# Slot steps of a fused transformer kernel: the feed-forward's norm on VectorE, the bias product behind the up product, activation tables loaded ahead

## The chip, the cores and the metric

The kernel is one program on one core of one Trainium2 chip. The metric is the device time of a run in microseconds (us), from first to last instruction with the launch around it. Before the change three runs gave 2456.42, 2447.18 and 2455.42 us; their median is 2455.42 us.

## The reference, cut to what matters

The whole reference is slot attention over a context, a routed mixture of experts, six transformer layers and a quantised feed-forward. Only the first part is touched. There 4 batches of 512 tokens of width 128 (the "slots") pass three times through this body:

```python
q = _ln(slots, lnq_g, lnq_b) @ wq + bq
logits = jnp.einsum('bnd,bkd->bnk', k, q) / scale
attn = jax.nn.softmax(logits, axis=-1) + EPS_ATTN
attn = attn / jnp.sum(attn, axis=1, keepdims=True)
upd = jnp.einsum('bnk,bnd->bkd', attn, v)
slots = upd @ wu + bu + prev
h = _ln(slots, lnm_g, lnm_b) @ w1 + b1
slots = jax.nn.gelu(h, approximate=False) @ w2 + b2 + slots
slots = _ln(slots + x_cls[:, None, :], lnp_g, lnp_b)
```

All of it is float32. The products with `wu` and the additions of `bu`, `b2` and `x_cls` are folded into prepared values (`slot_v`, `cond_rows`).

## The kernel before

`slot_steps` is unrolled: three steps (`s`), four batches (`b`), four tiles of 128 tokens per batch (`TB`). Each engine has its own in-order program, and semaphores that count up by one per batch tie them together: a wait holds everything behind it on that engine. The order within an engine is written out by hand as small software pipelines, `for k in range(B + 1 or B + 2)`, in which stage one works on batch `k`, stage two on `k - 1`, stage three on `k - 2`.

A step has two halves. In the **query half** TensorE turns the normalised state (`turn`, L311), multiplies with `wq` (L316) and with the keys (L320); ScalarE applies gain and offset (`gain`, L366), the query bias (L371) and the exponential (L375); VectorE takes the maximum and divides; TensorE makes the update (L327).

In the **feed-forward half**, which the change touches:

- VectorE's `add_update(s, b)` divides and adds the update (L488, L493) and takes the moments of the new state (L455 and L458) for all four batches in a row.
- GpSimd's `root_and_shift` makes from the moments of a batch the factor `rstd` (L410 and L413, a power of -0.5) and `shift` = -mean x rstd (L422, L425).
- ScalarE's `normal` (L381) makes `hat` = state x rstd + shift, four instructions per batch; then `gain` (L366) and `gelu` (L387). `normal` of batch `k`, `gain` of `k - 1` and `gelu` of `k - 2` follow each other.
- TensorE runs `turn` of batch `k` (L311), `up` of `k - 1` (L333) and `down` of `k - 2`. `down` waits for the gelu, then issues a product with one row of contraction that writes the bias (`ones32` with `cond_rows`, L337) into PSUM bank `2b`, and on top of it four products (L340). A float32 product is two matmul instructions in the trace.
- VectorE's `add_output` (L500) adds the result to the state and takes moments; GpSimd's `root` and VectorE's `normal` (L124) make the last norm one batch behind, and GpSimd's `last_gain` (L430, L431) applies its gain and offset. In steps 0 and 1 the moments, roots and norms of the next query (`query_moments`, `root`, `normal`) are woven in.

ScalarE holds one set of function tables at a time. The exponential and the gelu are in different sets, and the compiler puts an ACT_TABLE_LOAD in front of the first activation that needs another set; Identity needs none.

Of the kernel before, what the change touches and what calls it, by code (L numbers as in the profile page):

```python
# [14 lines left out]
ALU = mybir.AluOpType  # L15
# [275 lines left out]
def slot_steps(nc, a, m, sem):  # L291
# [13 lines left out]
    with nc.Block() as block:  # L305
        @block.tensor
        def _(pe):
            def turn(s, b, hat, turned):
                pe.wait_ge(hat, count(s, b))
                for t in range(TB):  # L310
                    last = nc.tensor.transpose(m.ps[:, 2 * b, t * P:(t + 1) * P], m.hat[:, b * TB + t, :], m.ident[:])  # L311
                last.then_inc(turned, 1)

            def queries(s, b):
                pe.wait_ge(in_q, count(s, b))
                nc.tensor.matmul(m.ps[:, 2 * b + 1, :], m.mats0[:, 2, :], m.xnT[:, b, :], start=True, stop=True).then_inc(q_ps, 1)  # L316

            def similarities(s, b):
                pe.wait_ge(q_sb, count(s, b))
                nc.tensor.matmul(m.ps[0:N_CTX, 2 * b, :], m.slot_k[:, b * N_CTX:(b + 1) * N_CTX], m.qT[:, b, :],  # L320
                                 start=True, stop=True).then_inc(logits, 1)

            def update(s, b):
                pe.wait_ge(attn, count(s, b))
                for t in range(TB):
                    bank, at = 2 * b + 1 - t // 2, t % 2 * 2 * P
                    last = nc.tensor.matmul(m.ps[:, bank, at:at + D + 1], m.attn[0:N_CTX, b, t * P:(t + 1) * P],  # L327
                                            m.slot_v[0:N_CTX, b, :], start=True, stop=True)
                last.then_inc(upd, 1)

            def up(s, b):
                pe.wait_ge(in_m, count(s, b))
                nc.tensor.matmul(m.ps[:, 2 * b + 1, :], m.mats0[:, 4, :], m.xnT[:, b, :], start=True, stop=True).then_inc(h_ps, 1)  # L333

            def down(s, b):
                pe.wait_ge(h_sb, count(s, b))
                nc.tensor.matmul(m.ps[:, 2 * b, :], m.ones32[0:1, :], m.cond_rows[0:1, b:b + 1, :].to_broadcast([1, TB, D]),  # L337
                                 start=True, stop=False)
                for t in range(TB):
                    last = nc.tensor.matmul(m.ps[:, 2 * b, t * P:(t + 1) * P], m.qT[:, b, t * P:(t + 1) * P], m.mats0[:, 5, :],  # L340
                                            start=False, stop=(t == TB - 1))
                last.then_inc(out_ps, 1)

            for s in range(SLOT_STEPS):
                for k in range(B + 2):
                    if k < B:
                        turn(s, k, hat_q, turned_q)
                    if 1 <= k <= B:
                        queries(s, k - 1)
                    if k >= 2:  # L350
                        similarities(s, k - 2)
                for b in range(B):
                    update(s, b)
                for k in range(B + 2):
                    if k < B:
                        turn(s, k, hat_m, turned_m)
                    if 1 <= k <= B:
                        up(s, k - 1)
                    if k >= 2:
                        down(s, k - 2)  # L360

        @block.scalar
        def _(act):
            def gain(s, b, turned, column, ready):
                act.wait_ge(turned, count(s, b))
                nc.scalar.activation(m.xnT[:, b, :], m.ps[:, 2 * b, :], ACT.Identity, bias=m.cols0[:, column + 1:column + 2],  # L366
                                     scale=m.cols0[:, column:column + 1]).then_inc(ready, 1)

            def query_bias(s, b):
                act.wait_ge(q_ps, count(s, b))  # L370
                nc.scalar.activation(m.qT[:, b, :], m.ps[:, 2 * b + 1, :], ACT.Identity, bias=m.cols0[:, 8:9]).then_inc(q_sb, 1)  # L371

            def exponentials(s, b):
                act.wait_ge(mx, count(s, b))
                nc.scalar.activation(m.attn[0:N_CTX, b, :], m.ps[0:N_CTX, 2 * b, :], ACT.Exp, bias=m.negmx[0:N_CTX, b:b + 1],  # L375
                                     scale=scale, accum_out=m.psum_rows[0:N_CTX, b:b + 1]).then_inc(probs, 1)

            def normal(s, b):
                act.wait_ge(root_m, count(s, b))
                for t in range(b * TB, (b + 1) * TB):  # L380
                    last = nc.scalar.activation(m.hat[:, t, :], m.state[:, t, :], ACT.Identity, bias=m.shift[:, t:t + 1],  # L381
                                                scale=m.st.rstd[:, t:t + 1])
                last.then_inc(hat_m, 1)

            def gelu(s, b):
                act.wait_ge(h_ps, count(s, b))
                nc.scalar.activation(m.qT[:, b, :], m.ps[:, 2 * b + 1, :], ACT.Gelu, bias=m.cols0[:, 9:10]).then_inc(h_sb, 1)  # L387

            for s in range(SLOT_STEPS):
                for k in range(B + 2):  # L390
                    if k < B:
                        gain(s, k, turned_q, 2, in_q)
                    if 1 <= k <= B:
                        query_bias(s, k - 1)
                    if k >= 2:
                        exponentials(s, k - 2)
                for k in range(B + 2):
                    if k < B:
                        normal(s, k)
                    if 1 <= k <= B:  # L400
                        gain(s, k - 1, turned_m, 4, in_m)
                    if k >= 2:
                        gelu(s, k - 2)

        @block.gpsimd
        def _(pool):
            chain = Chain(pool, pch)

            def add_epsilon(b):
                return nc.gpsimd.tensor_scalar(tiles(m.st.var, b), tiles(m.st.mv, b)[:, :, 1], LN_EPS, None, ALU.add)  # L410

            def power(b):
                return nc.gpsimd.tensor_tensor(tiles(m.st.rstd, b), tiles(m.st.var, b), m.minus_half[:], ALU.pow)  # L413

            def root(s, b, moments, ready):
                pool.wait_ge(moments, count(s, b))
                chain.link(add_epsilon(b))
                power(b).then_inc(ready, 1)

            def root_and_shift(s, b):  # L420
                pool.wait_ge(moments_m, count(s, b))
                nc.gpsimd.tensor_scalar(tiles(m.shift, b), tiles(m.st.mv, b)[:, :, 0], -1.0, None, ALU.mult)  # L422
                chain.link(add_epsilon(b))
                chain.link(power(b))
                nc.gpsimd.tensor_tensor(tiles(m.shift, b), tiles(m.shift, b), tiles(m.st.rstd, b), ALU.mult).then_inc(root_m, 1)  # L425

            def last_gain(s, b):
                pool.wait_ge(hat_p, count(s, b))
                hat = tiles(m.hat, b)
                chain.link(nc.gpsimd.tensor_tensor(hat, hat, m.rows0[:, 2:3, :].to_broadcast([P, TB, D]), ALU.mult))  # L430
                nc.gpsimd.tensor_tensor(tiles(m.state, b), hat, m.rows0[:, 3:4, :].to_broadcast([P, TB, D]), ALU.add).then_inc(gained, 1)  # L431

            for b in range(B):
                root(0, b, moments_q, root_q)
            for s in range(SLOT_STEPS):
                again = s + 1 < SLOT_STEPS
                for b in range(B):
                    root_and_shift(s, b)
                for k in range(B + 2):
                    if k < B:  # L440
                        root(s, k, moments_p, root_p)
                    if again and 2 <= k - 1:
                        root(s + 1, k - 3, moments_q, root_q)
                    if 1 <= k <= B:
                        last_gain(s, k - 1)
                if again:
                    root(s + 1, B - 1, moments_q, root_q)

        @block.vector
        def _(dve):  # L450
# [58 lines left out]
            for s in range(SLOT_STEPS):  # L509
                again = s + 1 < SLOT_STEPS  # L510
                for k in range(B + 1):
                    if k < B:
                        maximum(s, k)
                    if k >= 1:
                        divide(s, k - 1)
                for b in range(B):
                    add_update(s, b)
                for k in range(B + 1):
                    if k < B:
                        add_output(s, k)  # L520
# [1480 lines left out]
def build(nc, a):  # L2001
    with ExitStack() as ctx:
# [46 lines left out]
        m.invsum = {kind: sb(f"invsum_{kind}", [P, TB * 4, 2]) for kind in ("self", "cross")}  # L2049
        m.prefer = sb("prefer", [P, EXPERTS])  # L2050
        m.minus_half = sb("minus_half", [P, TB])
        m.slot_k = early(2400, NC_ALL)
        m.slot_vT = early(2750, NC_ALL)
        m.slot_v = early(3100, B, D + 1)
# [161 lines left out]
```

## Time and profile before

| | |
|---|---|
| median of 3 runs | 2455.42 us (2447.18 to 2456.42) |
| profiled execution | 2452.29 us, its span 2450.6 us |
| mean granted TensorE clock | 0.916 of full |
| busy over the span | PE 83%, PEld 37%, DVE 69%, ACT 63%, POOL 35% |
| DMA | 144.40 MB, mean 59 GB/s |
| ACT_TABLE_LOAD in the slot steps | 5: three before a gelu (L387), two before an exponential (L375) |

The span is that of the one core from its first to its last instruction; the profiled execution lasted 1.7 us more than its span. PE is TensorE's matmuls, PEld its weight loads, DVE VectorE, ACT ScalarE, POOL GpSimd. In a row of the timeline the first number is the start in us from the span's start, the second how long the merged instructions took together, xN their count, and the bracket says how long the engine had been idle before and what ended that.

### The profile page before, as it was taken

How to read it: one execution, taken by the hardware profiler on the slowest of the kernel's cores; microseconds unless marked ns; L12 is line 12 of the kernel's file. 1: busy time of each engine (PE TensorE's matmuls, PEld its weight loads, DVE VectorE, ACT ScalarE, POOL GpSimd, SP SyncE). 2: the span in 40 equal slices, each digit the busy share in tenths (PEclk: the TensorE clock that was granted, in tenths of full speed). 3: DMA queues.
4: the chain of work that ended last, by engine and by line, in shares of the span. 5: the costliest groups of instructions: out<-in, count | busy, mean ns of one | idle time of the engine just before them, and what ended most of it. 6: DMA issues, size and time to landing. Idle time of an engine off the chain costs nothing.

```text
span 2450.6 us, 38334 instructions
## 1 busy us (share of the span) xinstructions
PE 2035.4 (83%) x14066; PEld 899.4 (37%) x14066; DVE 1687.8 (69%) x3124; ACT 1539.8 (63%) x1939; POOL 857.1 (35%) x1354
## 2 busy tenths in 40 slices
PE   2654799926789999999999999999999999987652
PEld 1332576711223333333343333333333333332321
DVE  6776211136778888888878887888878887885455
ACT  1432233303567888788777888788778877867442
POOL 4443000012324444443444445434444445422321
PEclk9776899966999999999999999999999999988765
DMA  1000001032133334333333334333243334311100
GB/s 48 1 0 1 35 1 34 0 77 56 49 67 68 79 89 96 80 74 80 77 82 75 79 89 88 81 81 72 71 83 86 80 89 77 93 36 36 32 5 9
DMA packets 148642, 144.40 MB, mean 59 GB/s; under 512 B 30887, under 2 KB 136163, under 8 KB 148451
## 3 DMA queue, kind: packets, MB, share of 16 engines
q1 hardware_dynamic: 148463, 142.05, 25.9%
q8 instruction: 108, 1.77, 0.3%
q14 instruction: 71, 0.58, 0.1%
HBM read 79.01 MB, written 60.51 MB: 57 GB/s over the span
## 4 chain that ended last, share of the span: by engine, by line
PE 55%; DVE 14%; ACT 5%; issue 3%; POOL 1%; DMA 1%; SPq 0%; POOLq 0%; DVEq 0%; ACTq 0%
PE ps L1263 14%; PE ps L1227 6%; DVE smax L1761 6%; PE ps L1216 6%; PE ps L1341 5%; PE ps L1373 4%; PE ps L1382 4%; PE ps L1275 4%; ACT big L1496 2%; PE ps L1316 2%; DVE rot L1777 2%; PE ps L1300 2%; PE ps L1238 1%; PE ps L1250 1%; PE ps L1333 1%
## 5 line engine op out<-in xcount | busy, mean ns | idle before, releaser
L1496 ACT ACTIVATE big<-ps 128x1024 f32<-128x1024 f32 x960 | 955.4, 1026 | 275.2 <-PE ps L1227 253.5
L1761 DVE TENSOR_REDUCE smax<-ps 128x2 f32<-128x1024 f32 x768 | 921.6, 1221 | 264.2 <-PE ps L1216 258.4
L1263 PE MATMUL ps<-big,vaug 128*32 128x512 f32 x3072 | 414.3, 618 | 3.1 <-ACT big L1496 3.1
L1216 PE MATMUL ps<-k,q 49*128 49x512 bf16 x1536 | 294.3, 391 | 66.3 <-DVE smax L1761 35.4
L1227 PE MATMUL ps<-q,k 52*128 52x512 bf16 x1536 | 295.6, 388 | 29.0 <-DVE maxima L1768 13.1
L1692 POOL CAST mparts<-smax 128x16 bf16<-128x16 f32 x96 | 19.4, 202 | 573.1 <-DVE smax L1761 573.1
L1216 PEld LDWEIGHTS ps<-k,q 49*128 49x128 bf16 x1536 | 73.1, 94 | 313.5 <-DVE smax L1761 106.9
L694 DVE SCALAR_TENSOR_TENSOR state<-ps,share,state 128x128 f32<-128x128 f32 x128 | 36.0, 344 | 203.2 <-PE ps L665 203.2
L1768 DVE TENSOR_REDUCE maxima<-ps 128x8 f32<-128x616 f32 x192 | 144.8, 794 | 36.8 <-PE ps L1250 35.3
L682 ACT ACTIVATE big<-ps 128x512 f32<-128x512 f32 x128 | 76.4, 597 | 145.9 <-PE ps L656 145.9
L1341 PE MATMUL ps<-xnT,w 128*128 128x512 f32 x288 | 165.4, 660 | 0.9 <-ACT xnT L1533 0.9
L1227 PEld LDWEIGHTS ps<-q,k 52*128 52x128 bf16 x1536 | 75.5, 94 | 210.9 <-issue 92.4
L656 PE MATMUL ps<-xnT,big 128*128 128x512 f32 x256 | 120.0, 614 | 25.2 <-DMA big<-in_c_proj 25.2
L665 PEld LDWEIGHTS ps<-big 128*128 128x128 f32 x1024 | 119.1, 192 | 14.3 <-issue 14.3
L1683 POOL TENSOR_TENSOR hat<-rot,rparts 128x512 f32<-128x512 f32 x72 | 83.6, 1160 | 111.3 <-ACT rparts L1544 111.3
L665 PE MATMUL ps<-big 128*128 128x128 f32 x1024 | 119.2, 275 | 0.0
L1679 POOL TENSOR_TENSOR rot<-rot 128x512 f32<-128x512 f32 x72 | 91.4, 1269 | 74.1 <-DVE rot L1777 72.7
L1382 PE MATMUL ps<-w,hT 128*128 128x128 f32 x768 | 111.3, 290 | 4.5 <-ACT hT L1569 4.5
L1275 PE MATMUL ps<-big,vcaug 128*32 128x512 f32 x768 | 104.7, 616 | 11.0 <-DVE on_rows L1800 5.6
L1665 POOL TENSOR_SCALAR var_next<-mv_next 128x4 f32<-128x4 f32 x24 | 5.6, 233 | 309.4 <-DVE mv_next L1826 309.4
L1373 PE MATMUL ps<-xnT,w 128*128 128x512 f32 x192 | 108.3, 662 | 2.3 <-ACT xnT L1533 1.7
L1689 POOL TENSOR_TENSOR rparts<-hat,rparts 128x512 bf16<-128x512 f32 x72 | 83.3, 1158 | 75.2 <-ACT rparts L1548 75.2
(290 smaller groups left out, 3022.7 us busy)
## 6 DMA issues: line engine op xcount, KB each, us to landing
q<-scratch_queries SPq DMA_DIRECT2D x48, 384.0 KB, 6.1
k<-scratch_keys SPq DMA_DIRECT2D x48, 384.0 KB
cq<-scratch_cross_queries SPq DMA_DIRECT2D x48, 384.0 KB, 5.8
scratch_queries<-rparts SPq DMA_DIRECT2D x24, 384.0 KB, 2.4
scratch_keys<-rparts SPq DMA_DIRECT2D x24, 384.0 KB, 2.5
scratch_cross_queries<-rparts SPq DMA_DIRECT2D x24, 384.0 KB, 2.5
scratch_queries<-rparts SPq DMA_DIRECT2D x24, 256.0 KB, 2.7
scratch_keys<-rparts SPq DMA_DIRECT2D x24, 256.0 KB, 2.9
```

The source lines that it names most:

```text
L656: nc.tensor.matmul(m.ps[:, n % 4, :], m.fc[:, u, c * P:(c + 1) * P], m.xnT[:, b, :], start=True, stop=True).then_inc(h_ps, 1)
L665: last = nc.tensor.matmul(m.ps[:, 4 + i % 2, t * P:(t + 1) * P], m.hT[:, i % 2, c, t * P:(t + 1) * P], m.proj[:, u, c, :], start=(c == 0), ...
L1216: last = nc.tensor.matmul(out[:, u], m.q6[rows, v % 2, 2 * g + pr, qt * P:(qt + 1) * P], m.k6[rows, v % 2, 2 * g + pr, :], start=True, sto ...
L1227: last = nc.tensor.matmul(out[:, u], m.k6[rows, v % 2, 2 * g + pr, kt * P:(kt + 1) * P], m.q6[rows, v % 2, 2 * g + pr, :], start=True, sto ...
L1263: last = nc.tensor.matmul(m.ps[32 * j:32 * j + 32, pv_bank, :], of_head(m.vaug, v % 2 * TB + kt, g, j), of_quad("self", q)[:, j, :], start ...
L1275: last = nc.tensor.matmul(m.ps[32 * j:32 * j + 32, aux, :], of_head(m.vcaug, v % B, g, j), of_quad("cross", n)[:, j, :], start=(g % 2 == 0 ...
L1341: got = nc.tensor.matmul(banks(kind, i)[:, half, :], w_of(m, names[half]), m.xnT[:, xn[of_turn, i], :], start=True, stop=True)
L1373: nc.tensor.matmul(banks("up", 2 * v + c // 2)[:, c % 2], w_of(m, "f1")[:, c * P:(c + 1) * P], m.xnT[:, xn["ff", v], :], start=True, stop= ...
L1382: last = nc.tensor.matmul(m.ps[:, aux, t * P:(t + 1) * P], m.hT1[:, c, t * P:(t + 1) * P], w_of(m, "f2")[:, c * P:(c + 1) * P], start=(c = ...
L1496: nc.scalar.activation(of_quad(kind, p // 2)[:, p % 2 * 2:p % 2 * 2 + 2, :], banks("exp" if kind == "self" else "cross exp", p), ACT.Exp, ...
L1761: nc.vector.tensor_reduce(m.smax[:, n % 2, qt, :, pr], banks("max", i), AX.X, ALU.max).then_inc(s_read["self"], 1)
L1768: nc.vector.tensor_reduce(m.maxima[:, qt, :, PAIRS // 2 * half:PAIRS // 2 * (half + 1)], banks("cross max", i)[:, :, 0:PAIRS // 2 * N_CTX] ...
```

## The change

1. **The norm moves.** ScalarE's `normal` (48 instructions) goes away. VectorE's own `normal` (L124's form, with mean and rstd) now makes `hat` of batch `k - 1` behind `add_update` of batch `k`, waiting for `root_m`. GpSimd's `root_and_shift` becomes `root`: the two instructions that make `shift` go, the add and the power stay.
2. **The bias product moves.** L337's product is issued in `up(s, b)`, right behind the up product and ahead of `down(s, b - 1)`, instead of in `down(s, b)` behind its wait for the gelu.
3. **Tables.** A one-element activation on ScalarE (`load_table`) with Exp stands ahead of the first step and behind the gelus of steps 0 and 1, and one with Gelu behind the exponentials of every step, so that the table load falls there.
4. ScalarE's second pipeline has two stages, `gain(k)` and `gelu(k - 1)`, in place of three. A buffer `unused` of one column is added.

```diff
             def up(s, b):
                 pe.wait_ge(in_m, count(s, b))
                 nc.tensor.matmul(m.ps[:, 2 * b + 1, :], m.mats0[:, 4, :], ...).then_inc(h_ps, 1)
+                nc.tensor.matmul(m.ps[:, 2 * b, :], m.ones32[0:1, :], m.cond_rows[0:1, b:b + 1, :].to_broadcast([1, TB, D]),
+                                 start=True, stop=False)
             def down(s, b):
                 pe.wait_ge(h_sb, count(s, b))
-                nc.tensor.matmul(m.ps[:, 2 * b, :], m.ones32[0:1, :], m.cond_rows[0:1, b:b + 1, :].to_broadcast([1, TB, D]),
-                                 start=True, stop=False)
...
-            def normal(s, b):
-                act.wait_ge(root_m, count(s, b))
-                for t in range(b * TB, (b + 1) * TB):
-                    last = nc.scalar.activation(m.hat[:, t, :], m.state[:, t, :], ACT.Identity, bias=m.shift[:, t:t + 1],
-                                                scale=m.st.rstd[:, t:t + 1])
-                last.then_inc(hat_m, 1)
+            def load_table(function):
+                nc.scalar.activation(m.unused[0:1, :], m.minus_half[0:1, 0:1], function)
...
+            load_table(ACT.Exp)
             for s in range(SLOT_STEPS):
...
-                for k in range(B + 2):
+                load_table(ACT.Gelu)
+                for k in range(B + 1):
                     if k < B:
-                        normal(s, k)
-                    if 1 <= k <= B:
-                        gain(s, k - 1, turned_m, 4, in_m)
-                    if k >= 2:
-                        gelu(s, k - 2)
+                        gain(s, k, turned_m, 4, in_m)
+                    if k >= 1:
+                        gelu(s, k - 1)
+                if s + 1 < SLOT_STEPS:
+                    load_table(ACT.Exp)
...
-            def root_and_shift(s, b):
-                pool.wait_ge(moments_m, count(s, b))
-                nc.gpsimd.tensor_scalar(tiles(m.shift, b), tiles(m.st.mv, b)[:, :, 0], -1.0, None, ALU.mult)
-                chain.link(add_epsilon(b))
-                chain.link(power(b))
-                nc.gpsimd.tensor_tensor(tiles(m.shift, b), tiles(m.shift, b), tiles(m.st.rstd, b), ALU.mult).then_inc(root_m, 1)
...
                 for b in range(B):
-                    root_and_shift(s, b)
+                    root(s, b, moments_m, root_m)
...
-                for b in range(B):
-                    add_update(s, b)
+                for k in range(B + 1):
+                    if k < B:
+                        add_update(s, k)
+                    if k >= 1:
+                        normal(s, k - 1, root_m, hat_m)
```

## Rows read from the trace of the kernel before

**Rows 1.** Windows (busy us per engine, granted clock, DMA share, GB/s): the slot steps.
```profile
44.00:217.70 173.70, 102.09 (x384) 57.07 (x384) 120.68 (x518) 67.85 (x125) 81.11 (x120) 0.77 0.00 1
```

**Rows 2.** Timeline of step 1, VectorE, GpSimd and ScalarE around the updates.
```profile
122.68 0.22 DVE L488 RECIPROCAL colsum<-ps 128x2 f32<-128x2 f32 x2
...
125.30 0.20 DVE L488 RECIPROCAL colsum<-ps 128x2 f32<-128x2 f32 x2
125.47 0.24 POOL L422 TENSOR_SCALAR shift<-mv 128x4 f32<-128x4 f32 x1 [16.14 <-DVE mv L458]
...
127.44 1.65 ACT L381 ACTIVATE hat<-state,shift,rstd 128x128 f32<-128x128 f32 x4 [5.39 <-POOL shift L425]
```

**Rows 3.** Timeline of step 1, TensorE and ScalarE in the feed-forward half.
```profile
131.74 1.12 PE L311 MATMUL ps<-ident,hat 128*128 128x128 f32 x4 [1.48 <-ACT hat L381]
...
132.64 1.92 PE L333 MATMUL ps<-xnT,w 128*128 128x512 f32 x2
...
134.35 1.10 PE L311 MATMUL ps<-ident,hat 128*128 128x128 f32 x4
134.97 1.28 ACT L387 ACT_TABLE_LOAD   x1
136.27 0.69 ACT L387 ACTIVATE big<-ps,cols 128x512 f32<-128x512 f32 x1
137.00 1.12 PE L337 MATMUL ps<-cond_rows,ones 1*128 1x512 f32 x2 [0.20 <-ACT big L387]
139.05 0.60 PE L311 MATMUL ps<-ident,hat 128*128 128x128 f32 x4
139.49 1.02 PE L333 MATMUL ps<-xnT,w 128*128 128x512 f32 x2
140.44 1.12 PE L337 MATMUL ps<-cond_rows,ones 1*128 1x512 f32 x2
141.49 1.16 PE L340 MATMUL ps<-w,big 128*128 128x128 f32 x8
142.49 1.02 PE L333 MATMUL ps<-xnT,w 128*128 128x512 f32 x2
142.69 0.69 DVE L500 TENSOR_TENSOR state<-state,ps 128x512 f32<-128x512 f32 x1 [1.43 <-PE ps L340]
```

**Rows 4.** Timeline of step 1, the last norm on VectorE beside GpSimd.
```profile
144.62 1.09 DVE L124 TENSOR_SCALAR hat<-state,mv,rstd 128x128 f32<-128x128 f32 x4
144.79 0.23 POOL L410 TENSOR_SCALAR var<-mv 128x4 f32<-128x4 f32 x1 [2.09 <-DVE mv L458]
145.10 1.04 POOL L413 TENSOR_TENSOR rstd<-var,minus_half 128x4 f32<-128x4 f32 x1
145.69 0.69 DVE L500 TENSOR_TENSOR state<-state,ps 128x512 f32<-128x512 f32 x1
147.45 1.26 POOL L431 TENSOR_TENSOR state<-hat,w 128x512 f32<-128x512 f32 x1
147.62 1.95 DVE L124 TENSOR_SCALAR hat<-state,mv,rstd 128x128 f32<-128x128 f32 x4
```

**Rows 5.** Window from the last norm of step 1 to the next query, GpSimd alone.
```profile
143.00:163.70 20.70, 17.78 (x21) 0.59 0.00 0
```

**Rows 6.** Windows of 1 us in which TensorE's granted clock rises.
```profile
81.00:82.00 1.00, 1.00 (x3) 0.45 (x2) 0.00 (x0) 1.00 (x4) 0.00 (x0) 0.65 0.00 0
136.00:137.00 1.00, 0.81 (x2) 0.00 (x0) 0.00 (x0) 0.99 (x3) 0.00 (x0) 0.84 0.00 0
```

**Rows 7.** Timeline of step 0: turn of batch 1, `add_output` of batch 1.
```profile
75.60 1.11 PE L311 MATMUL ps<-ident,hat 128*128 128x128 f32 x4 [1.49 <-ACT hat L381]
...
87.00 0.69 DVE L500 TENSOR_TENSOR state<-state,ps 128x512 f32<-128x512 f32 x1 [1.43 <-PE ps L340]
```

**Rows 8.** Timeline of step 1, around ScalarE's first exponential.
```profile
115.06 0.15 DVE L475 TENSOR_SCALAR negmx<-rowmx 77x1 f32<-77x1 f32 x1
...
115.49 0.68 ACT L375 ACTIVATE big<-ps,negmx 77x512 f32<-77x512 f32 x1
```

More of the change, by code:

```diff
@@ L2051, in build @@
         m.minus_half = sb("minus_half", [P, TB])
+        m.unused = sb("unused", [P, 1])
         m.slot_k = early(2400, NC_ALL)
```

## The prediction

> **What bounds the kernel now.** I read the windows first, to see how much the change can touch: the slot steps take 173.70 us of the span, at a mean clock of 0.77; the rest of the span's 2450.6 us is left as it is [rows 1]. So the question is what sets the end of each of three short feed-forward halves. For that I read the timeline of step 1, which steps 0 and 2 repeat, in the order in which work is handed on.
>
> The updates: VectorE starts batch 0 at 122.68 and batch 1 at 125.30, so 2.60 us for each later one, with no wait [rows 2]. GpSimd answers the moments of batch 0 at 125.47 and ScalarE begins the norm at 127.44, done at 129.09 [rows 2]. The turns of batches 1 and 2, which follow their norms, start at 131.74 and 134.35 [rows 3].
>
> TensorE: from the turn of batch 1 at 131.74 on, it hardly stands idle: the one hole is 0.20 us ahead of the bias product at 137.00, which waited for the first gelu, and that had a table load of 1.28 us in front [rows 3]. Batch 1's result starts `add_output` at 142.69, after VectorE waited 1.43 us [rows 3].
>
> From there on the tail hangs on GpSimd: it waits 2.09 us for the moments of batch 1, starts at 144.79 [rows 4], and in the 20.70 us up to the next query it is busy for 17.78 us in 21 instructions, the rest mostly small gaps between them [rows 5]. The thing to see: **the end of a step follows the start of `add_output` of batch 1**, so each part is priced by what it does to that moment.
>
> **The norm on VectorE.** VectorE has no idle time between the updates, so a norm there pushes the later updates. Its price is that of the same instruction in the last norm: four tiles in 1.09 us, the next work 1.07 us after their start [rows 4]. GpSimd's root is quicker without the two shift instructions: 0.31 us from the add to the power and 1.04 for the power [rows 4]. That is 125.47 + 1.35 = 126.82, before VectorE is through with the second update at 127.90: no wait. Hence:
>
> - norm 0: 127.90 to 128.98 (before: 129.09);
> - update 2 from 128.97, norm 1: 131.57 to 132.65 (before, just ahead of the turn at 131.74);
> - update 3 from 132.64, norm 2: 135.24 to 136.32 (before, just ahead of 134.35);
> - norm 3 waits for the root of batch 3: GpSimd starts 2.79 us after the update, as in [rows 2], at 135.43, root at 136.78, norm done at 137.9.
>
> The moved work is 12 x 1.07 us on VectorE; in exchange 48 activations go, on an engine that is not late. The price is that batches 1 and 2 reach TensorE 0.95 and 2.0 us later. Queued behind `turn(2)`'s wait on TensorE are `up(1)`, its bias product and `down(0)`.
>
> **The bias product.** Its place in the order is the second price. Fast, one takes 1.05 us (140.44 to 141.49, [rows 3]). Before, batch 1's result needed two of them; now `up(2)` brings the third ahead of `down(1)`. A product that used to wait for a gelu hides nothing where TensorE is busy anyhow.
>
> **The sum on TensorE.** Slow durations, start to start: turn 0.90, up 1.71 (131.74, 132.64, 134.35); fast ones: turn 0.44, up 0.95, bias 1.05, down 1.00 (139.05, 139.49, 140.44, 141.49, 142.49) [rows 3]. No row has a bias product that is slow throughout: bounds 1.05 and 1.9 (1.71 and the 0.1 to 0.2 for its short weight load); I take 1.71, as it streams the same 512 columns as the up product.
>
> Turn 1 at 132.69; up 0 at 133.59; bias 0 at 135.30; turn 2 at 137.0 (its data came at 136.32, so no hole); up 1 at 137.9. The clock comes next. Before, it was at 0.84 in the window from 136 [rows 6], that is, rose near 136.3, 4.6 us after the turn of batch 1; in step 0 it is at 0.65 in the window from 81 [rows 6], so rose near 81.7, 6.1 us after the turn there at 75.60 [rows 7]. From 132.69 that gives 137.3 to 138.8. With the early rise: bias 1 at 138.85, down 0 at 139.9, turn 3 at 140.9, up 2 at 141.35, bias 2 at 142.3, down 1 at 143.35, and `add_output` of batch 1, which starts 1.20 us after `down` (141.49 to 142.69), at 144.55: 1.85 us later than before. With the late rise it is 0.4 us more; but step 0 had that rise before as well: its `add_output` came 11.40 us after the turn of batch 1, step 1's 10.95 [rows 3, 7]. So 1.85 again there, and I count step 2 as step 0. With the bias product's bounds, and rises mixed, one step costs between 0.8 and 2.5 us. Three steps: **+5.5 us** (2.4 to 7.5).
>
> **The tables.** The load before the gelu, 1.28 us in each of three steps, no longer stands there: its cover is the wait of ScalarE for the first turn. In the sum the gelu of batch 0 would be ready at 136.3 (up 0 over at 135.5, 0.69 us, [rows 3]) and is wanted by `down` at 139.9, so even with the load in place, at 137.6, nothing would wait: worth 0. The first exponential of step 1 starts at 115.49, behind its load, while its maximum was ready at 115.21 (115.06 + 0.15) [rows 8]: 0.24 us to gain with the handing on. Step 2, whose clock rose later in the query half, I count as nothing, and step 0 has no load there; the bounds are 0 and 3 x 0.24. The one-element activations are bounded by 0 and by the 0.69 us of a gelu of 512 columns each [rows 3], and lie where it waits for 5 us or more, after the exponentials [rows 2]; I take 0. By the Trainium skill (ScalarE: Activation LUTs, What ACT_TABLE_LOAD costs) a switch costs 1283 ns and a drain of about 1380 ns, 2.66 us; here the load starts at 134.97 and the gelu 1.30 us later, at 136.27 [rows 3], so the trace shows the first figure and no drain behind it. Rival C below would by the page's figure win 1.38 us more per step, 4.1 us in all.
>
> **Together**: 5.5 - 0.24 = +5.3 us. On the profiled execution, 2452.29 us (span 2450.6 and 1.7 around it), that makes 2457.6; it lies 3.1 us under the median of the runs, which becomes 2455.42 + 5.3 = **2460.7 us**, 0.22% more. A measurement of this kernel tells about 0.5%, 12.3 us, from no change.
>
> **The rivals.**
>
> *A, forecast: a small loss hidden in the spread.* TensorE and the late norms set the pace: 2460.7 us. Chance 0.70.
>
> *B, slower: the clock rises late.* TensorE now idles from 130.1 to 132.7 between the first two turns, where before it had 1.48 us between them [rows 3]. If the clock stayed at half until after `down(1)`: up 1 1.71, bias 1.71, down 2.0 (twice the fast 1.00), turn 0.9, up 1.71, bias 1.71 from 137.9 on give 147.6, and the result 2.1 us later: 149.8, 7.1 us late per step, 2455.4 + 21 = 2476 us. It passes 0.5% when a step loses 4.2 us: 5.25 us of lateness are spread over some 10 us of slow work, so 2.35 of them come with a rise at about 142, 9.3 us after the turn of batch 1. For it: the clock in the slot steps is often at half. Against: in both rises measured it took 4.6 to 6.1 us. Chance 0.10.
>
> *C, faster, inside the band: the table load was the path.* The hole at 137.00 was due to the first gelu, late by 1.28 us for its load [rows 3]. If VectorE's norms did not come later than ScalarE's, each step would win that 1.28 and the bias product of 1.05: 3 x 2.33 = 7.0 us, 2448.4 us. It needs the norm of batch 2 by about 134.3, and VectorE's queue gives 136.3. Chance 0.08.
>
> *D, VectorE's norm is slowed by GpSimd.* Beside the power of the root it took 1.09 us, beside the 512-column addition 1.95 [rows 4]. Were it 1.95 beside the root as well, the norm of batch 2 would be 3 x 0.87 = 2.6 us later, at 138.9, turn 2 1.9 us later: 3 x 1.9 = 5.7 us more, 2466.4 us. The row of 1.09 speaks against it: the power lay beside that one too. The Trainium skill (GPSIMD Engine Reference, Specifications) has the two engines share their SBUF interfaces, with contention for VectorE's two-port modes; the trace agrees beside the addition (1.95) and not beside the power (1.09). Chance 0.04.
>
> *E, outside the slot steps.* All later work is shifted against the clock's rises and falls, and a buffer of one column moves others. Up to 12 us either way would pass unseen; beyond the band I give 0.04 to each side.
>
> **The numbers.** Slower by over 0.5%: B's cases beyond 142, half of its 0.10 being beyond, with E's 0.04 and the chance 0.04 that the two medians drift apart by the 7 us that A lacks (the three runs spread over 9.2 us): 0.13. Faster: E's 0.04, and 0.02 of C with such a drift: 0.06. The rest, 0.81, is within. The range takes in C at 2448 and D at 2466 with some of B: 2448 to 2471 us; A alone, 2455 to 2466.
>
> **What would show it.** After: the norms (L124) between the updates at 1.1 us per batch; the turn of batch 2 some 14.3 us after the first reciprocal (L488) of the half, before 11.7; TensorE without a hole from the turn of batch 1 to `down(3)`; `add_output` of batch 1 21.9 to 22.3 us after that reciprocal, before 20.0 (142.69 less 122.68); the load of the gelu's table right behind the exponentials, with no wait of TensorE for it; GpSimd's tail of the same length. The prediction is wrong if the third bias product doesn't delay `down(1)`, if the turn of batch 2 isn't late, or if the tail doesn't follow `add_output` of batch 1.

## The result, and the profile after

The changed kernel takes 2461.26 us (median of 13 runs, 2456.39 to 2466.34), the kernel before, over all its 13 runs, 2451.71 us (2444.8 to 2456.42): a ratio of 1.0039, 95% interval 1.0029 to 1.0048, so 9.6 us more. A loss was forecast and came, inside the 0.5% below which the prediction sees no change, but nearly twice the 5.3 us of the sum. That the time itself lies only 0.6 us from the forecast 2460.7 is luck: the kernel before lies, over 13 runs, 3.7 us under the 2455.42 from which the forecast starts, and the larger loss made up for it. The profiled execution took 2460.35 us, its span 2458.4 us against 2450.6. Two of all the runs, one of `norm_only_rows` at 3262.77 us and one of `after_rows` at 7185.81 us, fell in a slow state and are in no ratio below.

The timeline of step 1, the counterpart of [rows 2, 3], on VectorE, GpSimd, ScalarE and TensorE; start, duration, instruction, idle time before it:

```profile
126.33 1.28 ACT L379 ACT_TABLE_LOAD   x1
126.94 0.23 DVE L479 RECIPROCAL colsum<-ps 128x2 f32<-128x2 f32 x2
129.57 0.20 DVE L479 RECIPROCAL colsum<-ps 128x2 f32<-128x2 f32 x2
...
132.17 1.08 DVE L124 TENSOR_SCALAR hat<-state,mv,rstd 128x128 f32<-128x128 f32 x4
...
135.79 1.08 DVE L124 TENSOR_SCALAR hat<-state,mv,rstd 128x128 f32<-128x128 f32 x4
...
136.93 1.12 PE L311 MATMUL ps<-ident,hat 128*128 128x128 f32 x4 [2.51 <-DVE hat L124]
...
137.84 1.92 PE L333 MATMUL ps<-xnT,w 128*128 128x512 f32 x2
...
139.42 1.08 DVE L124 TENSOR_SCALAR hat<-state,mv,rstd 128x128 f32<-128x128 f32 x4
...
139.69 2.07 PE L334 MATMUL ps<-cond_rows,ones 1*128 1x512 f32 x2
139.79 0.69 ACT L383 ACTIVATE big<-ps,cols 128x512 f32<-128x512 f32 x1 [0.93 <-PE ps L333]
...
141.69 1.11 PE L311 MATMUL ps<-ident,hat 128*128 128x128 f32 x4
...
144.44 2.07 PE L334 MATMUL ps<-cond_rows,ones 1*128 1x512 f32 x2
...
146.44 2.08 PE L340 MATMUL ps<-w,big 128*128 128x128 f32 x8
...
148.31 1.06 PE L311 MATMUL ps<-ident,hat 128*128 128x128 f32 x4
...
150.95 1.12 PE L334 MATMUL ps<-cond_rows,ones 1*128 1x512 f32 x2
...
152.00 1.16 PE L340 MATMUL ps<-w,big 128*128 128x128 f32 x8
...
153.19 0.69 DVE L491 TENSOR_TENSOR state<-state,ps 128x512 f32<-128x512 f32 x1 [2.63 <-PE ps L340]
```

Up to the turn of batch 1 it is the forecast to some hundredths: norms of 1.08 us, that turn 9.99 us after the first reciprocal (forecast 10.01). TensorE then has no hole. But every product up to 150 has the length of half clock: up 1.92, bias 2.07, down 2.08. `add_output` of batch 1 comes 26.25 us after the reciprocal, not 21.9. The windows of the same kernel, as [rows 6] (busy us per engine, then the granted clock third from the end), show the clock's rise in step 1 and, below it, in step 2:

```profile
150.00:151.00 1.00, 1.00 (x3) 0.05 (x1) 0.53 (x5) 0.19 (x1) 0.27 (x2) 0.59 0.03 8
151.00:152.00 1.00, 1.00 (x4) 0.24 (x3) 0.00 (x0) 0.69 (x1) 0.99 (x1) 1.00 0.00 0
201.00:202.00 1.00, 1.00 (x2) 0.50 (x2) 1.00 (x5) 0.68 (x1) 0.79 (x2) 0.50 0.00 0
202.00:203.00 1.00, 1.00 (x5) 0.35 (x4) 0.54 (x3) 0.01 (x1) 0.47 (x1) 0.99 0.00 0
```

In step 1 the upper level, 2.4 GHz, comes 14 us after the turn of batch 1 (136.93), in step 2 only 3.5 us after it (198.46). The steps between look alike otherwise, so I made one table for all kernels of the study, from their timelines and from windows of 0.5 us. Two levels occur, 1.2 GHz (0.50 in the windows) and 2.4 GHz (1.00). "Half" is the time from the first reciprocal of the feed-forward half to `add_output` of batch 1, in steps 0, 1, 2; "rise" is when, by these windows, the clock reaches the upper level, less the start of the turn of batch 1, good to some 0.3 us. Ratios are to the kernel before, timed beside each kernel.

| kernel | half, us | rise, us | ratio (95%) |
|---|---|---|---|
| before | 20.5, 20.0, 20.4 | 5.9, 4.8, 6.1 | 1 |
| changed | 26.3, 26.3, 21.3 | 14.2, 14.1, 3.5 | 1.0039 (1.0029 to 1.0048) |
| norm_only | 27.0, 27.0, 27.1 | none in any step | 1.0073 (1.0056 to 1.0091) |
| bias_only | 22.5, 22.5, 22.4 | 8.3, 8.1, 8.0 | 1.0028 (1.0012 to 1.0044) |
| tables_only | 20.0, 19.7, 20.5 | 5.3, 4.6, 6.1 | 0.9984 (0.9973 to 0.9995) |
| after_filler | 23.6, 26.3, 26.2 | 8.2, 14.1, 14.0 | 1.0054 (1.0036 to 1.0071) |
| norm_only_rows | 22.1, 21.9, 21.9 | 8.1, 7.7, 7.6 | 1.0022 (1.0010 to 1.0034) |
| after_rows | 20.7, 21.0, 20.2 | 4.6, 5.1, 3.4 | 1.0005 (0.9995 to 1.0016) |
| before_rows | 19.5, 19.4, 19.4 | 5.5, 4.7, 4.2 | 0.9993 (0.9982 to 1.0005) |
| tables_rows | 19.1, 19.1, 19.1 | 4.7, 4.7, 5.1 | 0.9964 (0.9949 to 0.9978) |
| after_behind | 22.4, 22.1, 22.1 | 8.5, 8.0, 7.8 | 1.0017 (1.0006 to 1.0029) |
| after_behind_rows | 19.6, 19.4, 19.4 | 4.1, 3.5, 3.8 | 0.9971 (0.9962 to 0.9981) |
| tables_behind_rows | 19.1, 19.1, 19.1 | 5.1, 5.0, 4.9 | 0.9952 (0.9933 to 0.9971) |
| norm_only_32 | 22.4, 22.4, 20.8 | 6.9, 7.3, 3.7 | 1.0052 (1.0031 to 1.0072) |

**Where the time went.** In the two profiles the three halves grew by 5.9 + 6.2 + 0.9 = 13.0 us. The stretches up to the first half and from `add_output` of batch 1 to the next half shrank by 1.3, 0.3 and 1.3 us, the last tail (18.07 to 18.05 us) did not move. So the slot steps end 10.1 us later (217.77 to 227.83). The unchanged rest took 2230.6 us in place of 2232.8; in the 14 profiles of the study it lies anywhere from 2226.4 to 2236.1 us, which is why single spans don't decide here.

### The profile page after: what moved, and what is told of

The parts are those of the page before. It is cut to its first block, busy times and chain, and to the rows that moved or that the text cites. A ratio compares the mean times of both kernels' runs of the same rounds, so it can differ in the third digit from the quotient of the medians.

```text
span 2458.4 us, 38312 instructions
## 1 busy us (share of the span) xinstructions
PE 2044.4 (83%) x14062; PEld 902.4 (37%) x14066; DVE 1699.3 (69%) x3172; ACT 1522.5 (62%) x1897; POOL 850.8 (35%) x1330
## 4 chain that ended last, share of the span: by engine, by line
PE 54%; DVE 13%; ACT 5%; issue 3%; POOL 2%; DMA 1%; SPq 0%; POOLq 0%; DVEq 0%; ACTq 0%
PE ps L1257 13%; PE ps L1221 6%; DVE smax L1755 6%; PE ps L1210 6%; PE ps L1335 5%; PE ps L1367 4%; PE ps L1376 4%; PE ps L1269 4%; ACT big L1490 3%; DVE rot L1771 2%; PE ps L1310 2%; PE ps L1294 2%; PE ps L1232 1%; PE ps L1244 1%; PE ps L1327 1%
## 5 line engine op out<-in xcount | busy, mean ns | idle before, releaser
L1686 POOL CAST mparts<-smax 128x16 bf16<-128x16 f32 x96 | 19.4, 202 | 574.4 <-DVE smax L1755 574.4
L659 PEld LDWEIGHTS ps<-big 128*128 128x128 f32 x1024 | 119.1, 192 | 14.3 <-issue 14.3
```

Of the source, the lines that this page charges most:

```text
L659: last = nc.tensor.matmul(m.ps[:, 4 + i % 2, t * P:(t + 1) * P], m.hT[:, i % 2, c, t * P:(t + 1) * P], m.proj[:, u, c, :], start=(c == 0), ...
```

## The experiments

**1. The three parts alone, and a filled hole.** `norm_only` undoes the bias product's move and the early tables in the changed kernel; `bias_only` and `tables_only` make one of these in the kernel before:

```diff
 # norm_only, against the changed kernel
 def up(s, b):
     ...
-    nc.tensor.matmul(m.ps[:, 2 * b, :], m.ones32[0:1, :], m.cond_rows[0:1, ...], start=True, stop=False)
 def down(s, b):
     pe.wait_ge(h_sb, count(s, b))
+    nc.tensor.matmul(m.ps[:, 2 * b, :], m.ones32[0:1, :], m.cond_rows[0:1, ...], start=True, stop=False)
...
-            load_table(ACT.Exp)
...
-                load_table(ACT.Gelu)
```

```diff
 # after_filler, against the changed kernel
+            def filler():
+                nc.tensor.matmul(m.ps[:, 1, :], m.mats0[:, 4, :], m.mats0[:, 0:4, :], start=True, stop=True)
...
                     if k < B:
                         turn(s, k, hat_m, turned_m)
+                    if k == 0:
+                        filler()
```

> Only the norm moves to VectorE (GpSimd without the shift); the bias product and the table loads stay where they were. Theory (late norms, clock): the turn of batch 2 starts 13.6 us or more after the first reciprocal of the feed-forward half (11.7 before), and add_output of batch 1 comes 2 to 5 us later than before in each step, 6 us more if the clock rises late; time +4 to +9 us on the kernel before. Rival (the bias product placed ahead of down makes the loss): within 2 us of the kernel before.

> Only the bias product moves behind the up product; norm on ScalarE, table loads as before. Theory (one more product stands ahead of down(1), TensorE has no hole to hide it): add_output of batch 1 some 0.9 us later per step than the 20.0 to 20.5 us of before, time +2 to +4 us. Rival (the product fills the wait for the gelu): add_output not later, time -2 to 0 us.

> Only the one-element activations that load the tables early; all else as before. Theory (the load in front of the first gelu made only a hole of 0.2 us on TensorE): -0.2 to -0.7 us per step, time -2 to 0 us. Rival (the load is on the path): -1.3 us per step, -4 us.

> The changed kernel, with one product of 512 columns more per step on TensorE between the turns of batches 0 and 1, into a bank that up(0) overwrites; it fills most of the 2.5 us in which TensorE waits there. Theory (that wait lets the clock rise late, 13.6 us after the turn of batch 1 in step 1): the rise comes within 7 us of that turn in each step, add_output of batch 1 lies 21.3 to 22.5 us after the first reciprocal in all three steps (26.3 in steps 0 and 1 of the changed kernel), time 4 to 9 us under the changed kernel's. Rival (the loss is the late norms and the third bias product alone): the steps stay at 26 us and the time within 2 us of the changed kernel's, 1.0039 of before.

Measured: `norm_only` 2470.07 us beside 2452.67, 1.0073: 17.4 us, nearly twice the highest loss expected. The parts don't add up: by the ratios 17.9 and 6.9 us are lost and 4 us won in each part alone, 9.6 us lost with all three. `bias_only` moved the half by 2.0 to 2.4 us, not by 0.9, and came to 1.0028, more than the 2 to 4 us expected; its clock, too, rose late, after 8.0 to 8.3 us. `tables_only` won 0.9984, the whole of what its rival said, but its halves are only 0.4, 0.3 and 0 us shorter, and its slot steps as a whole 1.9 us; the rest of the 4 us lies where nothing was changed, within what profiles differ by there. `after_filler` missed: the hole was filled (the wait for the turn of batch 1 went from 2.51 to 0.80 us) and the rise came after 8.2, 14.1 and 14.0 us, earlier than in the changed kernel in step 0, as there in step 1, later in step 2, and in no step within the 7 us expected; the time is 1.0054. So my theory that the idle time between the first two turns delays the clock fell.

The timeline of `norm_only`, step 1, TensorE, shows what did not fit it (the last row is a window, with the granted clock third from the end):

```profile
140.25 1.11 PE L311 MATMUL ps<-ident,hat 128*128 128x128 f32 x4 [2.51 <-DVE hat L124]
141.15 1.91 PE L333 MATMUL ps<-xnT,w 128*128 128x512 f32 x2
143.88 1.12 PE L311 MATMUL ps<-ident,hat 128*128 128x128 f32 x4 [0.81 <-DVE hat L124]
144.78 1.92 PE L333 MATMUL ps<-xnT,w 128*128 128x512 f32 x2
146.63 2.07 PE L337 MATMUL ps<-cond_rows,ones 1*128 1x512 f32 x2
148.63 2.08 PE L340 MATMUL ps<-w,big 128*128 128x128 f32 x8
150.50 1.06 PE L311 MATMUL ps<-ident,hat 128*128 128x128 f32 x4
...
164.92 2.08 PE L340 MATMUL ps<-w,big 128*128 128x128 f32 x8
165.00:166.00 1.00, 1.00 (x5) 1.00 (x6) 1.00 (x5) 0.00 (x0) 0.80 (x2) 0.50 0.00 0
```

From 143.88 to 167.0 TensorE has work without a hole, 23 us long, and the clock never rises: the window from 165 still has 0.50, and so does every other of that half. The order of the products is that of the kernel before: there, too, a turn, an up, a turn and an up come first (131.74 to 136.8, [rows 3]), but without a hole, and the clock had risen, near 136.3, by the start of the first bias product at 137.00. Here the late norm leaves a hole of 0.81 us ahead of the turn of batch 2; the first bias product starts 6.4 us after the turn of batch 1, not 5.3, and the clock is still down when it does. What follows is again the same order, and the clock stays down. What sets the bias products apart is that they have a single row of contraction (`1*128` in the row), all others of this half 128. So they became the suspect.

**2. The bias product over 128 partitions.** Every partition of `cond_rows` holds the bias, so the identity as weights gives the same value:

```diff
-nc.tensor.matmul(m.ps[:, 2 * b, :], m.ones32[0:1, :], m.cond_rows[0:1, b:b + 1, :].to_broadcast([1, TB, D]), ...)
+nc.tensor.matmul(m.ps[:, 2 * b, :], m.ident[:], m.cond_rows[:, b:b + 1, :].to_broadcast([P, TB, D]), ...)
```

> norm_only with the bias product contracted over all 128 partitions (the identity against the bias rows, which every partition holds) in place of one partition; same value, same columns, same place. In norm_only the clock never rose in the feed-forward halves, though TensorE worked for 22 us without a hole. Theory (with one row of contraction the bias product does little for the clock, so a half in which it stands between the others stays slow): the clock rises in every step within 7 us of the turn of batch 1; add_output of batch 1 at 21 to 22.5 us after the first reciprocal (27.04 in norm_only); time 14 to 20 us under norm_only, 0.999 to 1.002 of before. Rival (only the phase of the rise, not the product): 26 to 27 us in most steps, time within 5 us of norm_only.

> The changed kernel with the bias product over 128 partitions. Theory: add_output of batch 1 at 21 to 22 us in all three steps (26.3, 26.3, 21.3 in the changed kernel), time 7 to 12 us under the changed kernel, 0.999 to 1.001 of before; what stays over before is the 1.3 us of late norms and third product per step. Rival (phase): as the changed kernel, 1.003 to 1.005.

> The kernel before with the bias product over 128 partitions. Theory: there the clock had risen at or before the first bias product in two of three steps, so little is left: add_output of batch 1 at 19.7 to 20.2 us, time -2 to 0 us. Rival: the same, 0.

> The kernel before with the tables loaded early and the bias product over 128 partitions; the norm stays on ScalarE, the bias product in down. Theory: the gain of tables_only (-4 us, 0.9984) and at most 1 to 2 us more, 0.997 to 0.9985 of before. Rival (the two gains are the same one): 0.998 to 1.0.

Measured: `norm_only_rows` 2457.86 us beside 2451.41, 1.0022, its clock up 7.6 to 8.1 us after the turn in all steps, its halves 5 us shorter than `norm_only`'s. That is the expected direction by somewhat less than the expected size (a rise within 7 us, 14 to 20 us under `norm_only`; by the ratios it is 12.5). `after_rows` 1.0005: no loss is left that the interval would show, with rises after 3.4 to 5.1 us. `before_rows` 0.9993, inside the noise, and `tables_rows` 0.9964, somewhat better than expected. The timeline of `norm_only_rows`, step 1, TensorE, the same order as above:

```profile
137.93 1.11 PE L311 MATMUL ps<-ident,hat 128*128 128x128 f32 x4 [0.80 <-DVE hat L124]
138.83 1.92 PE L333 MATMUL ps<-xnT,w 128*128 128x512 f32 x2
140.54 1.69 PE L337 MATMUL ps<-cond_rows,ident 128*128 128x512 f32 x2
142.07 1.05 PE L340 MATMUL ps<-w,big 128*128 128x128 f32 x8
...
144.26 1.02 PE L337 MATMUL ps<-cond_rows,ident 128*128 128x512 f32 x2
145.12 1.05 PE L340 MATMUL ps<-w,big 128*128 128x128 f32 x8
```

`down` takes 1.05 us at once: the clock rose near 141.9, some 1.4 us after the first bias product had begun, where `norm_only`'s stayed down for good. The rival, that only the moment had changed at which the clock's own course meets the half, does not explain this. All six runs of `norm_only` lie at 2465.9 to 2473.8 us, all eleven of `norm_only_rows` at 2454.6 to 2461.6. And where the clock had fallen equally far ahead of the turn of batch 1, it still rose at different times: in step 0 of `after_filler` (one partition) it fell 5.3 us ahead and rose 8.3 us behind, in step 1 of `after_rows` it fell 5.2 us ahead and rose 5.1 us behind. But the moment counts too: in step 2 of the changed kernel and of `after_rows` alike it fell 6.7 us ahead and rose some 3.5 us behind, 0.8 us after the start of the first bias product, and there its form made no difference.

`norm_only_rows` and `after_rows` show one thing more. With the product moved ahead (and the tables early), the hole of 0.80 us ahead of the turn of batch 2 is gone, and the clock rises after 3.4 to 5.1 us in place of 7.6 to 8.1.

A second, smaller gain is in the last two rows above: from its start to the next product the bias takes 0.86 us (144.26 to 145.12), with one partition 1.05 [rows 3]. At half clock it is 1.70 with 128 partitions (in `after_rows`, from 136.03 to 137.73) against 2.00 in the changed kernel (141.69 less 139.69 above).

**3. Its place, with the new form and the old.** The bias product goes behind `down` of the batch before, in the changed kernel with one partition (`after_behind`) and with 128 (`after_behind_rows`), and with the norm left on ScalarE, early tables and 128 partitions (`tables_behind_rows`):

```diff
                     if 1 <= k <= B:
                         up(s, k - 1)
                     if k >= 2:
                         down(s, k - 2)
+                    if 1 <= k <= B:
+                        bias(s, k - 1)
```

> The changed kernel with the bias product over 128 partitions and issued behind down of the batch before instead of ahead of it. Theory (in the changed kernel one more product than needed stands ahead of down(1)): add_output of batch 1 some 0.9 us earlier than the 20.2 to 21.0 us of after_rows, add_output of batch 2 about as there; time 1 to 3 us under after_rows, 0.999 to 1.0003 of before. Rival (the place among the products does not matter): 1.0005 as after_rows.

> A candidate for the best version: norm on ScalarE as before, tables loaded early, bias product over 128 partitions and issued behind down of the batch before. Theory: at the start of the half TensorE has hardly a hole, so taking the bias product out of down wins at most 0.9 us per step for batch 1 and costs it elsewhere; 0 to 2 us under tables_rows, 0.9955 to 0.9965 of before. Rival (the product now delays the turns of batches 2 and 3): 0 to 3 us over tables_rows.

> The changed kernel with the one-partition bias product issued behind down of the batch before. Theory (the one-partition product keeps the clock down wherever it stands among the first products): at least one step of three with add_output of batch 1 over 24 us; time 0.5 to 3 us under the changed kernel, 1.0025 to 1.004 of before. Rival (only its place was wrong): add_output at 20 to 21.5 us in all steps, 1.000 to 1.001.

Measured: `after_behind_rows` 2445.14 us beside 2451.58, 0.9971, 6.4 us under before with the norm on VectorE, and its halves 0.8 to 1.6 us shorter than `after_rows`'. By the ratios it is 8.3 us under `after_rows`, where 1 to 3 were expected and the three halves give 3.5; the rest is not traced. `after_behind` 1.0017: the theory asked for a step over 24 us and there is none. The rises come at 7.8 to 8.5 us, so a product with one partition does not keep the clock down for 14 us wherever it stands; but the halves are 2.7 to 2.8 us longer than those of its twin with 128 partitions. `tables_behind_rows` is the fastest of all, 2440.86 us, 0.9952; its interval and that of `tables_rows` overlap and their halves are equal, so the place of the product is not shown to matter there. Their timelines agree with that: in both `add_output` waits 1.04 us for batch 1, in a half of 19.1 us. `tables_behind_rows`, step 1:

```profile
129.01 1.11 PE L311 MATMUL ps<-ident,hat 128*128 128x128 f32 x4 [1.49 <-ACT hat L385]
...
131.63 1.91 PE L336 MATMUL ps<-cond_rows,ident 128*128 128x512 f32 x2
...
134.91 1.05 PE L342 MATMUL ps<-w,big 128*128 128x128 f32 x8
...
139.05 0.69 DVE L510 TENSOR_TENSOR state<-state,ps 128x512 f32<-128x512 f32 x1 [1.04 <-PE ps L342]
```

**4. Rows or length?** The form with 128 partitions changes two things: the rows, and the pause behind the product. `norm_only_32` takes 32 partitions, and so leaves out the bias for 96 of every 128 tokens:

```diff
+nc.tensor.matmul(m.ps[:, 2 * b, :], m.ident[0:32, :], m.cond_rows[0:32, b:b + 1, :].to_broadcast([32, TB, D]), ...)
```

> norm_only with the bias product contracted over 32 partitions (the first 32 rows of the identity and of the bias rows); it leaves out the bias for 96 of every 128 tokens, the number and size of the instructions stay. It is to split two differences of the 128-partition form: the rows of contraction, and the product's length, 2.0 us from start to start at half clock with one partition, 1.70 with 128. If the pause behind the product is what holds the clock down, the clock rises here whenever the product takes 1.70 us, and stays down when it takes 2.0. If the rows do it, the clock can stay down with a product of 1.70 us. Times: 1.002 of before if the clock rises in all steps as in norm_only_rows, 1.007 if it never rises as in norm_only.

Measured: no answer for either. In the profiled execution (2452.82 us) the clock rose in all three steps, after 3.7 to 7.3 us, and the product kept its longer form. But the clock rose before that product could show what it does. Step 1, then the window of the rise (granted clock 0.74), then two rows of step 2:

```profile
139.63 1.41 PE L337 MATMUL ps<-cond_rows,ident 32*128 32x512 f32 x2
...
141.97 0.60 PE L311 MATMUL ps<-ident,hat 128*128 128x128 f32 x4
...
143.36 1.12 PE L337 MATMUL ps<-cond_rows,ident 32*128 32x512 f32 x2
144.41 1.16 PE L340 MATMUL ps<-w,big 128*128 128x128 f32 x8
...
140.00:140.50 0.50, 0.50 (x2) 0.13 (x1) 0.00 (x0) 0.43 (x1) 0.00 (x0) 0.74 0.00 0
...
191.32 1.12 PE L311 MATMUL ps<-ident,hat 128*128 128x128 f32 x4 [2.51 <-DVE hat L124]
...
194.95 0.66 PE L311 MATMUL ps<-ident,hat 128*128 128x128 f32 x4 [0.80 <-DVE hat L124]
```

(143.36 to 144.41 is 1.05 us, as with one partition.) In step 1 the first bias product had run for 0.6 us when the clock rose, near 140.3; in step 2 the turn of batch 2 already has the length of the upper level, and no bias product of that half had run. Up to the first bias product the work is that of `norm_only`, whose clock did not rise there: the same work was followed by a rise in one execution and not in another.

The ten runs fall into two groups: 2452.8, 2452.9, 2456.2, 2456.7, 2460.2 and 2465.6, 2466.8, 2467.4, 2467.5, 2468.6 us, the second at the level of `norm_only` (2465.9 to 2473.8 in six runs), the first at that of `norm_only_rows` (2454.6 to 2461.6 in eleven). That the upper group is the executions in which the clock stays down is likely from its level, but no profile of it was taken. So 32 rows are shown to be neither as safe as 128 nor always as slow as one, and whether the rows or the pause decide stays open.

## Why the prediction was right, and what was off

- **The norm's queue on VectorE**: right, 1.08 us a batch. The turn of batch 1 started 9.99 us after the first reciprocal (forecast 10.01). The data of batch 2 came as forecast: in `norm_only` its turn starts at 13.61 us (forecast 13.64). In steps 0 and 1 of the changed kernel that turn started at 14.75, not 14.3, because at half clock the bias product took 2.00 us from start to start and not 1.71, and the up product ahead of it 1.85 and not 1.71: the upper bound of 1.9 for the bias product was just too low.
- **GpSimd's root** came in time, and no contention from it (rival D): the three norms between and behind the updates have 1.08 us each, each beside a power on GpSimd; D did not occur.
- **The third bias product ahead of `down(1)`**: right. Moved behind `down`, it won 0.8 to 1.6 us a half with 128 partitions. With an early rise the changed kernel's step 2 lost 0.9 us, less than the 1.85 of the sum, since there the rise came after 3.5 us.
- **The clock's rise** is the mis-sized term. The forecast took 4.6 to 6.1 us from the turn of batch 1, "in both rises measured". It measured 14.2, 14.1 and 3.5 us. Two late rises cost some 5 us each (26.3 against 21.3), so that the halves lost 13.0 us and not 5.5. This is rival B in part, which had a chance of 0.10. Its price was nearly right: for a rise 9.5 us later than the sum's it gives 1.85 + 9.5 x 5.25 / 10 = 6.8 us, and the two steps lost 5.9 and 6.2. The halves alone lost more than the 12.3 us that are 0.5%; the time stayed inside because the stretches between them shrank by 2.9 us, which was not forecast. B's reason, the idle time between the first two turns, was wrong: filling it won nothing. What the runs show in its place is the bias product of one row, which meets the half while the clock is still down: because the change puts it among the first products (`bias_only`), or because the late norms hold the rise back until it comes (`norm_only`). With 128 rows at the same place the late rises are gone (1.0039 to 1.0005, 1.0073 to 1.0022).
- **The tables**: their worth in the changed kernel was not measured. Alone, in the kernel before, they are worth 0.16% with an interval of 0.05 to 0.27%, 1.2 to 6.6 us, against 0.24 us in the sum, which was made for the changed order, where the gelu is not awaited. In the kernel before, the one hole of 0.20 us closed (in `tables_only` the first bias product follows the up product at once). The changed kernel's gelu starts 0.93 us after the end of its last work and waits for the up product, not for a table: there the 0 holds. Rival C (the load is the path) would need the norms to be early, and they were not.
- **The tail** follows `add_output` of batch 1 in all kernels but `norm_only`: 18.04 to 18.09 us from it to the end of the slot steps. In `norm_only`, where the clock is down throughout, it is 20.0 us: there VectorE waits another 2.71 and 1.00 us for the results of batches 2 and 3, so TensorE, not GpSimd, sets the tail.
- What made the total come nearer than the halves: in the query halves the clock rose earlier in two steps, 1.3 us each, which nothing in the change explains; the start of the first half lies anywhere from 65.1 to 66.5 us in the 14 profiles.

## What to carry to other kernels

Before a wait is filled with a product from elsewhere, ask what stands in line behind it: one product more than needed ahead of a result delays it, here by 0.8 to 1.6 us (`after_rows` against `after_behind_rows`). Where short bursts of products follow idle stretches, price each burst at both clock levels, and look at what the products ahead of the rise are: a bias product over one partition cost more than its length here, and the same value over all 128 partitions took it back (1.0005 in place of 1.0039, nothing else changed; where the norm had not moved and the clock rose early anyway, it won nothing clear of noise, 0.9993). Moving a norm to an engine whose queue sets the order costs its full length for every later batch, however idle the engine that it leaves: here 0.9 us for batch 1 and 1.9 us for batch 2.

## What was not expected of the hardware

- TensorE had work for 23 us without a hole and was granted only 1.2 GHz (`norm_only`, 143.88 to 167.0), in a stretch that all three steps have alike. With the bias products' contraction over 128 partitions in place of one, the same order had 2.4 GHz after 7.6 to 8.1 us, and the time fell from 1.0073 to 1.0022 of before. The Trainium skill (TensorE: Matmul & The Clock Gate, What's actually happening) has the half clock as the default that activity lifts and idle time brings back. In the changed kernel each fall in the slot steps lies in an idle stretch of TensorE (near 130.4, with the engine idle from 128.2 to 133.3), as the page says; the 23 us of work at half clock differ from it, and the measurement decides.
- The clock also fell in the middle of work. In the kernel before, step 1, TensorE, with one-row bias products and `down` in turn:

```profile
143.44 1.12 PE L337 MATMUL ps<-cond_rows,ones 1*128 1x512 f32 x2
144.49 1.16 PE L340 MATMUL ps<-w,big 128*128 128x128 f32 x8
145.58 1.14 PE L337 MATMUL ps<-cond_rows,ones 1*128 1x512 f32 x2
146.00:147.00 1.00, 1.00 (x3) 0.36 (x2) 0.97 (x4) 0.00 (x0) 1.00 (x2) 0.78 0.00 0
147.00:148.00 1.00, 1.00 (x6) 1.00 (x6) 0.97 (x7) 0.00 (x0) 0.92 (x2) 0.50 0.00 0
```

  The last two rows are windows: the granted clock goes from 1.00 to 0.78 and 0.50 with TensorE busy all the time, and the next `down`, from 146.65 on, takes 2.08 us in place of 1.16. The same happened twice in `tables_only` (near 90.1 and 144.7). In the slot steps of the six kernels with 128 partitions no fall lies in a stretch of work. This fits the bias products' single row; it does not tell the row from the pause.
- A float32 product of 512 columns with one or 32 rows of contraction takes 1.05 us from start to start at the upper level and, with one row, 2.00 at the lower, one with 128 rows 0.86 and 1.70.
- Open: whether the number of rows, their contents, the weights (ones or the identity) or the pause behind the product decide. Open too: why one order sometimes rises after 3.5 and sometimes after 14 us. In steps 0, 1 and 2 of the changed kernel the clock had fallen 6.4, 6.6 and 6.7 us ahead of the turn of batch 1 and rose 14, 14 and 3.5 us behind it, so a small shift between the work and the clock's own course may be enough; no run was made to show it.
